# Rotation of queries ahead of key work, and the causal mask written by VectorE from step 12 on: one fused attention and feed-forward block on one core

## What is computed

```python
q = rms_norm((ln(x) @ wq).reshape(B, 64, 16, 128), q_norm_w)     # 16 heads of 128
k, v = ln(x) @ wk, ln(x) @ wv                                    # 4 kv heads; k normalized likewise
k_ctx, v_ctx = ctx @ wk_ctx, ctx @ wv_ctx                        # context keys normalized, not rotated
q = q * cos + rotate_half(q) * sin;  k = k * cos + rotate_half(k) * sin
scores = q @ concat(k_ctx, k).T / sqrt(128) + causal mask on the self part
x = x + tanh(g_xattn) * (softmax(scores) @ concat(v_ctx, v)) @ wo
fuse = silu(ln(x) @ fp8(gate_w) * gate_scale) * (ln(x) @ fp8(up_w) * up_scale)
x = x + tanh(g_ffn) * (fuse @ fp8(down_w)) * down_scale
```

## Time and profile before

| | |
|---|---|
| median of 3 runs | 312.32 us (312.31 to 313.82) |
| the profiled execution | 312.29 us, of which span 310.2 us |
| TensorE, granted clock | full speed in every slice |
| busy share of the span: PE, PEld, DVE, ACT, POOL | 95%, 76%, 74%, 75%, 58% |
| chain that ended last, by engine | PE 31%, ACT 27%, DVE 25%, issue 8%, POOL 6% |
| mean of one: GpSimd's add of rotated queries (L1395), ScalarE's copy of x2's high part (L898) | 1.281 us, 0.398 us |

### The profile page before, as it was taken

How to read it: one execution, slowest core, us unless ns; L and a number is a source line. 1 busy time by engine, 2 the same in 40 slices (tenths; PEclk the granted TensorE clock), 3 DMA queues, 4 the chain that set the end, 5 groups by cost and what they waited for, 6 DMA issues and landing times.

```text
span 310.2 us, 6558 instructions
## 1 busy us (share of the span) xinstructions
PE 294.8 (95%) x2231; PEld 234.8 (76%) x2231; DVE 229.4 (74%) x481; ACT 232.2 (75%) x893; POOL 180.8 (58%) x177
## 2 busy tenths in 40 slices
PE   6896989998999999999999999999999999988876
PEld 3354656675877888888888888888888888877765
DVE  1668998889888898769875787758775976676553
ACT  2468687887789978888977768787887778776632
POOL 1225695567747687457955586457755685556330
PEclk9999999999999999999999999999999999999999
DMA  6999000000000010000000010000000000000001
GB/s 200 389 389 394 15 17 2 0 1 2 18 3 0 1 36 2 0 0 21 19 0 2 0 37 0 2 1 20 0 3 0 2 17 4 2 0 19 0 0 36
DMA packets 6720, 12.84 MB, mean 41 GB/s; under 512 B 800, under 2 KB 4256, under 8 KB 6688
## 3 DMA queue, kind: packets, MB, share of 16 engines
q1 hardware_dynamic: 6688, 12.43, 11.3%
HBM read 11.38 MB, written 1.05 MB: 40 GB/s over the span
## 4 chain that ended last, share of the span: by engine, by line
PE 31%; ACT 27%; DVE 25%; issue 8%; POOL 6%; DMA 2%; SPq 1%; DVEq 0%; POOLq 0%
ACT probs L932 10%; ACT squares L768 6%; PE ps_y L444 5%; DVE row_max L1217 4%; DVE exp_bias L1220 3%; DVE q_sin L1082 3%; PE ps_attn L737 3%; PE ps_transposed L430 3%; ACT qt L852 3%; PE ps_scores L693 3%; DVE q_rot L1078 2%; PE ps_kv L418 2%; ACT const L825 2%; PE ps_probs L430 2%; DMA const<-in_constants_dram 2%
## 5 line engine op out<-in xcount | busy, mean ns | idle before, releaser
L932 ACT ACTIVATE probs<-ps_scores,exp_bias,q_scale 128x128 f32<-128x128 f32 x128 | 57.0, 456 | 26.5 <-DVE exp_bias L1220 26.4
L1395 POOL TENSOR_TENSOR q_rot<-q_rot,q_sin 128x512 f32<-128x512 f32 x31 | 39.7, 1281 | 17.6 <-DVE q_sin L1082 17.5
L1439 POOL TENSOR_TENSOR probs<-probs,row_inv 128x512 f32<-128x512 f32 x32 | 36.3, 1134 | 19.0 <-DVE row_inv L1273 19.0
L1346 POOL TENSOR_TENSOR q_scale<-ssq_eps,minus_half 128x4 f32<-128x4 f32 x32 | 38.8, 1213 | 10.5 <-DVE ssq_eps L1243 9.8
L1357 POOL TENSOR_TENSOR fuse_lo<-fuse,fuse_hi 128x256 fp32r<-128x256 f32 x21 | 15.4, 733 | 41.8 <-ACT fuse_hi L777 41.8
L768 ACT ACTIVATE squares<-ps_q 128x128 bf16<-128x128 f32 x128 | 34.1, 292 | 5.9 <-PE ps_q L412 4.1
L737 PE MATMUL ps_attn<-pt,values 128*128 128x256 f32 x128 | 33.4, 383 | 0.0
L693 PE MATMUL ps_scores<-kt,qt 128*64 128x128 f32 x512 | 33.3, 273 | 0.0
L1078 DVE TENSOR_TENSOR q_rot<-ps_q,rope 128x512 f32<-128x512 f32 x31 | 21.2, 684 | 11.9 <-ACT squares L768 11.9
L693 PEld LDWEIGHTS ps_scores<-kt,qt 128*64 128x64 f32 x512 | 28.9, 137 | 0.0
L908 ACT ACTIVATE pt<-ps_probs 128x512 f32<-128x512 f32 x32 | 19.2, 600 | 11.8 <-PE ps_probs L430 11.6
(11 more groups left out here) (190 smaller groups left out, 832.0 us busy)
## 6 DMA issues: line engine op xcount, KB each, us to landing
q_raw<-in_wq_dram SPq DMA_DIRECT2D x4, 512.0 KB, 8.7
o_raw<-in_wo_dram SPq DMA_DIRECT2D x4, 512.0 KB, 11.6
ctx_t<-in_ctx_dram SPq DMA_DIRECT2D x8, 128.0 KB, 2.6
out_dram<-x_sb SPq DMA_DIRECT2D x8, 128.0 KB, 1.9
stage<-in_gate_w_dram SPq DMA_DIRECT2D x2, 384.0 KB, 10.4
stage<-in_up_w_dram SPq DMA_DIRECT2D x2, 384.0 KB, 11.4
x_sb<-in_x_dram SPq DMA_DIRECT2D x1, 768.0 KB, 13.4
stage<-in_down_w_dram SPq DMA_DIRECT2D x2, 384.0 KB, 13.1
```

The lines of the kernel that those rows point to most:

```text
L932: last = nc.scalar.activation(probs[:, i, :], ps_s[:, i * P:(i + 1) * P], ACT.Exp, bias=exp_bias[:, i:i + 1], scale=q_scale[:, k % 2, i:i ...
L1346: return nc.gpsimd.tensor_tensor(dst, src, minus_half[:, 0:src.shape[1]], ALU.pow)
L1395: nc.gpsimd.tensor_tensor(q_rot[:, :, :], q_rot[:, :, :], q_sin[:, :, :], ALU.add)\
L1439: nc.gpsimd.tensor_tensor(probs[:, :, :], probs[:, :, :], row_inv[:, :].unsqueeze(2).broadcast_to([P, 4, P]), ALU.mult).then_inc(probs_rea ...
```

## The change

Two things change. First, VectorE rotates the queries of step k+1 as soon as their product is made, ahead of the work on keys, of the token normalization at j = 3 and of the feed-forward gating; ScalarE squares them after that instead of before, GpSimd adds them ahead of its feed-forward and key work, TensorE's next product of queries waits for the squares, and ScalarE's copy of x2's high part stands ahead of its squares of self keys. Second, from step 12 on VectorE copies a ready-made mask of 128 x 128 into the four heads' places of the scores' bank, after the exponentials of the step before have read it; TensorE leaves its mask matmuls out and adds the scores onto that.

```diff
+MASK_ON_VECTOR_FROM = 12
...
@@ TensorE, one_step
                     if is_step(u, k):
-
-                        pe.wait_ge(q_sin_ready, step(u, k) + 1)
-                    if at_step(u, k) == 0:
-                        pe.wait_ge(q_squared, 1)
+                        pe.wait_ge(q_squared, step(u, k) + 1)
...
-                    for r in range(2):
+                    if step(u, k) >= MASK_ON_VECTOR_FROM:
+                        pe.wait_ge(mask_set, step(u, k) - MASK_ON_VECTOR_FROM + 1)
+                    for r in range(2 if step(u, k) < MASK_ON_VECTOR_FROM else 0):
...
@@ ScalarE, square_queries
-                    act.wait_ge(q_made, step(u, k + 1) + 1)
+                    act.wait_ge(q_sin_ready, step(u, k + 1) + 1)
...
@@ VectorE
+            def fill_mask():
+
+                dve.wait_ge(mask_cleared, 1)
+                for r in range(2):
+                    rows = slice(r * LEN, (r + 1) * LEN)
+                    last = nc.vector.tensor_copy(mask_all[rows, rows], const[rows, C_MASK:C_MASK + LEN])
+                last.then_inc(mask_filled, 1)
+
+            def set_mask(s):
+
+                if s == MASK_ON_VECTOR_FROM:
+                    dve.wait_ge(mask_filled, 1)
+                dve.wait_ge(exp_ready, s)
+                nc.vector.tensor_copy(four(ps_s), mask_all[:, :].unsqueeze(1).broadcast_to([P, HPG, P])).then_inc(mask_set, 1)
...
@@ rotate_queries
-                    dve.wait_ge(q_squared, step(u, k + 1) + 1)
+                    dve.wait_ge(q_made, step(u, k + 1) + 1)
...
@@ VectorE, one_step: behind x2's normalization
+                rotate_queries(u, k)
+
                 if j == 3 and is_tile(u, m + 2):
...
-
-                rotate_queries(u, k)
...
+                    dve.wait_ge(q_squared, step(u, k + 1) + 1)
                     nc.vector.tensor_scalar(ssq_eps[:, :], ssq[:, :], DIM * RMS_EPS, None, ALU.add)\
...
                     nc.vector.reciprocal(row_inv[:, :], row_sum[:, :]).then_inc(inv_ready, 1)
+                    if is_step(u, k + 1) and step(u, k + 1) >= MASK_ON_VECTOR_FROM:
+                        set_mask(step(u, k + 1))
...
@@ GpSimd, one_step: ahead of fuse_rest and of the keys' add
+                if is_step(u, k + 1):
+                    pool.wait_ge(q_sin_ready, step(u, k + 1) + 1)
+                    nc.gpsimd.tensor_tensor(q_rot[:, :, :], q_rot[:, :, :], q_sin[:, :, :], ALU.add)\
+                        .then_inc(q_rot_ready, 1)
```

More of the change, by code:

```diff
@@ L112, in build @@
         ident_bf = sb("ident_bf", [P, P], bf16)
+        mask_all = sb("mask_all", [P, P])
         ident = const[:, C_ID:C_ID + P]
@@ L209, in build @@
         half_set = sem("half_set")
+        mask_cleared, mask_filled, mask_set = sem("mask_cleared"), sem("mask_filled"), sem("mask_set")
         tables_ready = sem("tables_ready")
@@ L876, in one_step @@
                     fuse_high(u, FF_LATE.get(k - 1))
+                if j == 2 and is_tile(u, m - 1):
+                    act.wait_ge(x2_turned, tile(u, m - 1) + 1)
+                    nc.scalar.activation(x2t[0][:, (m - 1) % 2, :, :].rearrange("p c n -> p (c n)"), ps_t[:, 0:HID], ACT.Copy)\
+                        .then_inc(x2_hi_ready, 1)
                 if j == 2 and is_tile(u, m + 1):
@@ L895, in one_step @@
                             .then_inc(xt_hi_ready, 1)
[L896 to L899, removed]
                 if j == 3 and is_tile(u, m + 1):
@@ L1339, in _ @@
             scales()
+            fill_mask()
             run_steps(dve, one_step)
@@ L1390, in one_step @@
                         .then_inc(ks_added, 1)
-                if is_step(u, k + 1):
-                    pool.wait_ge(q_sin_ready, step(u, k + 1) + 1)
-                    nc.gpsimd.tensor_tensor(q_rot[:, :, :], q_rot[:, :, :], q_sin[:, :, :], ALU.add)\
-                        .then_inc(q_rot_ready, 1)
                 if ROUND_AT.get(k - 1, 0) >= WIDE:
@@ L1460, in _ @@
             nc.gpsimd.memset(minus_half[:, :], -0.5).then_inc(half_set, 1)
+            nc.gpsimd.memset(mask_all[:, :], 0.0).then_inc(mask_cleared, 1)
             first_roots()
```

## The result

The changed kernel takes 317.54 us (median of 4 runs, 317.48 to 320.34) against 312.31 (312.3 to 313.82) measured beside it: ratio 1.0178, 95% interval 1.015 to 1.0207. It is slower, by 5.2 us, where 3.5 were forecast.

What follows compares the result with a forecast made beforehand. TensorE's queue was taken as the bound in steps 12 to 28. Losses 4.8 + 0.7 + 1.7 + 0.5 = 7.7 less gains 2.6 + 1.6 = 4.2 gave 312.3 + 3.5 = 315.8 us, range 311.5 to 319.5.

Steps and rivals of the forecast that it cites:

- The bound: Steps 12 to 28: TensorE's queue is the limit; other engines count only where they hand something over late.
- j = 2: Steps 14, 18, 22, 26: TensorE stands 1.2 us for squared self keys, 4.8 in all; step 10 adds 0.7.
- j = 1: Normalized context keys come late: 0.5 us each in steps 17, 21, 25, 0.1 in 13 and 9; 1.7 lost.
- Steps 0 to 8: Step 1's wait for keys grows by 1.20 us, mostly swallowed in steps 3 and 6: 0.5 lost, bounds -0.5 and 2.2.
- The mask off TensorE: Removing two mask matmuls gains 0.13 us in each of 20 steps from 12 on, 2.6 us in all.
- The copy: VectorE's mask copy from step 12, ahead of the attention output's low part: 0.6 us a step, costing TensorE 0.
- The tail: Last four steps: earlier exponentials recover 1.6 us of TensorE's 2.4 us of waits in steps 29 to 31; bounds 0.8, 2.4.
- Collision: Rival, chance 0.12: VectorE's mask copy waits for GpSimd's multiplication of probabilities, 1.13 us on average; 5 us more, 320.8.
- Even: Rival, chance 0.15: stalls are half as long, and masks and last four steps pay for them; 312.3 us, within 1.5.
- Faster: Rival, chance 0.12: a chain through other engines, not TensorE, sets the step; near 302 us, or 308 with smaller gains.
- the ring of exponentials: Cycle of exponentials, turned queries, scores, maximum and bias, supposed to set the step; it loses VectorE's 11.9 us wait for squares.

Runs made afterwards that it cites:

- the order alone: Changed kernel with the mask back on TensorE in all steps, its new order of rotation and squares kept: 320.36 us, ratio 1.0233 against the kernel before.
- the kernel with the copy of x2 moved: Changed kernel with ScalarE's copy of x2's high part put ahead of its squares of queries in step 30 alone: median 319.19 us.

## Why the prediction was right, and where it was off

**The bound.** Right, nearly. TensorE's queue had hardly any room from step 12 to 28, and each handover with little slack became a wait of TensorE. The rows without waits hid a little: with the mask on TensorE as before, but the rotation early at j = 3 and 0, step 16 lasts 8.37 for 8.42 and step 17 9.02 for 9.13.

**j = 2.** Right, in mechanism and size. Forecast 1.2 us of standing; from the turned probabilities to the context values it is 1.63 (184.34 to 185.97) where it was 0.41 before (182.00 to 182.41), 1.22 more. The row itself shows 0.96, since an end of a matmul is modelled. The old order at j = 2 took 6.5 us back (317.5 to the 311.0 at full clock), somewhat more than the five steps' 5.25.

**j = 1.** Right in the changed kernel: 0.33 net of the mask in each of three steps, 0.37 forecast, by the chain I had written, 3.27 us for 3.19. That it is 0.33 and not the whole 1.20 of the rotation comes from before: `k_var` began only 0.72 after the product ended (170.95, 170.23). The root is one of two limits of nearly the same length: in step 17 the normalization waited 0.16 for it. With `k_var` taken out of the rotation's way, VectorE's own queue is the other.

**Steps 0 to 8.** Right in sum (+0.45), and partly by luck. The wait in step 1 grew by 1.19 (1.33 to 2.52), as forecast, but TensorE had come to step 1 0.75 earlier and turned the keys only 0.11 later (29.96 for 29.85). Step 3 gave its 0.90 back, as forecast. I had not seen that step 0 would gain 0.84, nor that step 5 would lose 0.87 (a new wait of 0.64 for the same keys); and step 6, which was to swallow lateness too, grew by 0.24. The two parts that I had not seen cancel.

**The mask off TensorE.** Mis-sized: "0.13 us of TensorE for each of the 20 steps" is the start distance of mask and scores, and 0.07 to 0.08 is what the pair is worth, since the scores behind it are shorter. At j = 3 these 0.08 are all that was gained. At j = 0 a step gained 0.16, of which 0.05 are there in the kernel with the order alone, so the row came out near its forecast, -0.92 for -1.04, with a part that I had put at nothing.

**The copy.** Right in the changed kernel: 0.667 to 0.679 us in 20 places, and hidden. In 17 of them GpSimd's multiplication runs beside it for 0.06 to 0.52 us and takes its 1.04 all the same, so there is no collision. The Trainium skill, "VectorE: DVE Perf Modes", section "Why PSUM operands drop a tier", says that an operand in PSUM rules out the mode that needs both read ports of SBUF; this case's trace agrees. I took 0.60, which is the distance of two rotations; as a row also a rotation reads 0.68.

**The tail.** This is the step that failed, most of the 1.8 us between 315.8 and 317.5: "I take 1.6 of it back". The three waits of the earlier trace rows do hang on the exponentials, but they aren't independent. The first (0.83 for `qt`, step 29) went. In the same step the rotation ahead of the gating made `fuse_hi`, and so `fuse_lo`, late by 0.90; with the old order at j = 1 that wait is gone. It in turn hid the second wait. The third grew from 0.74 to 1.30, because "the copy of x2's high part and GpSimd's adds, also moved, end long before TensorE needs them" holds for TensorE and not for VectorE: the maximum of step 30 stands behind `x2t_lo`, and this behind the copy. Measured: 0.55 back, masks included, for 2.12; this is below even the 0.8 that I had as the lower bound for the waits alone.

**Rivals.** *Collision*: no. *Even*: the stalls were not half. *Faster*: the stall in j = 2 is not below 0.4, so the ring of exponentials does not set the full steps. But a part of this rival is there: an early rotation at j = 0 and 3, which holds nobody up, gives some 2.6 of the 3.4 us by which the kernel with the old order at j = 1 and 2 is faster than the kernel before. Through which engine `ot_lo` and the keys come earlier there, no run takes apart.

Open: whether the clock's fall in step 1 (below) follows from the longer wait, and what the 1.4 to 1.5 us more around the span are in some runs.

## What to carry to other kernels

Work that is moved forward to where its input is made must be costed by what it passes: here 1.2 us of rotation ahead of keys with 0.17 (j = 2) and 0.06 us (j = 1) of slack cost 1.2 and 0.3 a step, the latter because the keys' own work had begun late anyway, while at j = 0 and 3, where nobody waits behind it, the same move gained. Of several waits in a row that hang on one thing, count only the first as recoverable until a trace shows more, and follow its followers on the other engines too, since the next wait takes over what the first gives up. The value of an instruction taken out of a full queue is the change of distance between its neighbours, with the next instruction's length beside it, and not its start distance.

## What the hardware showed

TensorE's clock fell in step 1 in two profiled runs of the four kernels that stand 2.52 us for `k_sin` there; in the other two, the changed kernel's among them, it stayed at 1.00. The windows of one of them, the kernel with the copy of x2 moved (stretch, length, busy of TensorE, its weight load, VectorE, ScalarE and GpSimd, granted clock, transfers):

```profile
28.00:30.00 2.00, 0.02 (x1) 0.03 (x1) 0.88 (x4) 1.94 (x10) 1.81 (x2) 0.79 1.03 397
30.00:32.00 2.00, 2.00 (x6) 1.48 (x7) 1.90 (x6) 1.30 (x3) 1.55 (x2) 0.50 0.64 227
32.00:34.00 2.00, 2.00 (x3) 0.75 (x3) 1.27 (x3) 1.59 (x8) 0.30 (x2) 0.50 0.03 11
34.00:36.00 2.00, 2.00 (x6) 1.24 (x5) 1.59 (x2) 0.00 (x0) 1.54 (x1) 0.51 0.00 0
36.00:38.00 2.00, 2.00 (x9) 1.01 (x7) 0.00 (x0) 1.08 (x2) 0.00 (x0) 1.00 0.00 0
```

The granted clock went to 0.50 (1.2 of 2.4 GHz) while TensorE stood, and stayed there until 36 us; step 1 lasted 12.90 us instead of the 9.95 of the changed kernel's profile. In the other run, with the old order at j = 2, the wait ended at 30.73; the clock reads 1.00 from 28 to 30 us, 0.68 to 32 and 0.50 to 34, and step 1 lasted 11.61. Of the runs of the four kernels with this wait of 2.52 us 12 in 22 had a mean clock of 0.995 or less; of the five with waits of 0.28 and 1.33 and none else in this step, none in 20; of four that keep the order of before in steps 0 and 1 (waits of 0.66, 0.46 and 1.33), 7 in 34, and of the kernel before itself, with the same waits, 7 in 45, where I haven't seen the place. So a wait that is swallowed later on paper may still cost 1.7 to 3 us of clock. That is a count: the four kernels differ from the others in more than this wait, and no experiment on its length was made.
